# Expert tiles in groups of four, two and two rows, a new mix of step kinds, and two areas for tile outputs

## Time and profile before

| | us |
|---|---|
| median of 3 runs | 3298.54 (3296.21 to 3299.12) |
| profiled execution | 3306.1 |
| its span, first to last instruction | 3303.9 |
| mean granted TensorE clock | 0.959 |
| VectorE busy | 2989.0 (90%) |
| TensorE busy | 2864.8 (87%) |
| ScalarE busy | 2649.0 (80%) |
| GpSimd busy | 2656.7 (80%) |

### The profile page before, as it was taken

One profiled execution on the slowest core, in us unless ns is written; L12 is line 12 of the kernel. 1 busy time (PEld: TensorE's weight loads), 2 busy tenths in 40 slices (PEclk: granted clock), 3 DMA queues, 4 the chain that ended last, 5 costly groups with the idle time before them and its releaser, 6 DMA issues.

```text
span 3303.9 us, 58893 instructions
## 1 busy us (share of the span) xinstructions
PE 2864.8 (87%) x21429; PEld 2595.6 (79%) x21429; DVE 2989.0 (90%) x2141; ACT 2649.0 (80%) x6150; POOL 2656.7 (80%) x1289
## 2 busy tenths in 40 slices
PE   6889898988988799999868899989878879999676
PEld 5888888887877689888766788888767778899566
DVE  6999999999989999999999999999999999999610
ACT  6878888887978799898968689897977879988322
POOL 4889999888978898888988789797888878877501
PEclk8999999999999999999989899999989999999788
DMA  3342222222222335334221243524221143454176
GB/s 109 99 157 87 66 64 78 65 64 69 69 58 62 90 126 166 113 105 141 89 72 48 78 147 119 162 91 148 71 70 52 56 127 119 153 159 136 53 252 214
DMA packets 264660, 347.51 MB, mean 105 GB/s; under 512 B 88218, under 2 KB 157603, under 8 KB 263988
## 3 DMA queue, kind: packets, MB, share of 16 engines
q1 hardware_dynamic: 260418, 332.98, 32.5%
q0 software_dynamic: 3072, 8.39, 0.7%
q10 hardware_dynamic: 882, 2.38, 0.2%
HBM read 313.03 MB, written 30.62 MB: 104 GB/s over the span
## 4 chain that ended last, share of the span: by engine, by line
PE 33%; ACT 21%; DVE 17%; issue 14%; POOL 13%; DMA 2%; SPq 1%; DVEq 0%; POOLq 0%; ACTq 0%
POOL hC L1065 11%; ACT dA L1260 10%; DVE h L1292 9%; PE psY L1606 9%; PE psG L1545 8%; PE psX L1587 4%; DVE psX L1282 4%; PE psG L1632 4%; ACT xs L1231 3%; PE psX L1577 3%; PE psX L1545 2%; ACT gT L1114 1%; ACT hid L1215 1%; PE psX L1569 1%; DMA w_up<-in_w_exp 1%
## 5 line engine op out<-in xcount | busy, mean ns | idle before, releaser
L1065 POOL TENSOR_TENSOR hC<-h,cb 128x1024 f32<-128x1024 f32 x1024 | 2402.0, 2368 | 436.3 <-DVE h L1292 426.1
L1292 DVE TENSOR_TENSOR_SCAN h<-dA,psX 128x1024 f32<-128x1024 f32 (+1 forms) x1115 | 2303.7, 2101 | 83.4 <-ACT dA L1260 20.9
L1260 ACT ACTIVATE dA<-dt,negA 128x255 f32<-128x255 f32 x4096 | 1729.8, 510 | 180.1 <-DVE h L1292 178.4
L1606 PE MATMUL psY<-ident,hC 128*128 128x128 f32 x8192 | 1102.6, 279 | 47.9 <-DVE gT L1307 35.1
L1606 PEld LDWEIGHTS psY<-ident,hC 128*128 128x128 f32 x8192 | 956.3, 144 | 64.3 <-DVE gT L1307 38.2
L1282 DVE TENSOR_TENSOR psX<-dtu,psX 128x1024 f32<-128x1024 f32 x443 | 535.7, 1209 | 19.1 <-PE psX L1569 18.0
L1577 PE MATMUL psX<-ident,xs 128*128 128x128 f32 x2992 | 409.9, 282 | 115.2 <-ACT xs L1231 62.1
L1231 ACT ACTIVATE xs<-dtuT,bT 128x512 f32<-128x512 f32 x748 | 500.0, 723 | 1.3 <-PE psX L1577 1.2
L1577 PEld LDWEIGHTS psX<-ident,xs 128*128 128x128 f32 x2992 | 346.6, 145 | 169.4 <-ACT xs L1231 81.9
L1587 PE MATMUL psX<-diag_b,dtuT 128*128 128x128 f32 x3312 | 423.3, 282 | 39.2 <-DVE h L1292 37.4
L1587 PEld LDWEIGHTS psX<-diag_b,dtuT 128*128 128x128 f32 x3312 | 402.6, 197 | 68.5 <-issue 64.9
(11 more groups left out here) (213 smaller groups left out, 2056.7 us busy)
## 6 DMA issues: line engine op xcount, KB each, us to landing
cb<-c_dram SPq DMA_DIRECT2D x256, 512.0 KB
w_up<-in_w_exp SPq DMA_DIRECT2D x201, 256.0 KB, 3.1
w_down<-in_w_exp SPq DMA_DIRECT2D x201, 256.0 KB, 3.0
diag_b<-b_dram SPq DMA_DIRECT2D x207, 128.0 KB, 3.6
dA<-in_w_exp SPq DMA_DIRECT2D x39, 256.0 KB, 5.4
h<-in_w_exp SPq DMA_DIRECT2D x39, 256.0 KB, 5.2
x_slots<-got SPq DMA_DIRECT2D x16, 512.0 KB, 5.0
xg<-x_slots SPq DMA_DIRECT2D x60, 128.0 KB, 3.0
```

The costliest lines, as they stand in the source:

```text
L1065: eng.tensor_tensor(hC[i % NHC][:, :, :], h[i % NH][:, :, :], cw.to_broadcast([P, KI, L]), ALU.mult).then_inc(times_c, 1)
L1260: made = eng.activation(dA[j % NA][:, c, 1:L], dt[n % 2][:, c, 1:L], ACT.Exp, scale=negA[:, JOBS[n][0], c, s:s + 1])
L1292: made = eng.tensor_tensor_scan(h[i % NH][:, part, :].rearrange("p c t -> p (c t)"), dA[i % NA][:, part, :].rearrange("p c t -> p (c t)"), ...
L1606: made = eng.matmul(psY[:, tc, c * P:(c + 1) * P], hC[i % NHC][:, c, tc * P:(tc + 1) * P], ident[:, :], start=s == 0 and c == 0, stop=s == ...
```

## The change

The first ten jobs have the mix `EARLY`, the last six a new `LATE` with 26 P, 13 M and 25 T. Rows 0 to 3 are one group (23 tiles), rows 4 and 5 and rows 6 and 7 are two groups of 15. The slots of an area double (`SLOTS` = 8 * 1024), and `y_slots` becomes two areas by the group's parity, so that a group's first store waits only for the rows of the group before the last; 64 clearing DMAs of 512 KB replace 24. In the tail, the output tasks of rows 4 and 5 are taken from where they were put, and all set as one block behind the second product of the sixth tile of the last group.

```diff
-LATE = "PTPMPTPTPMTPTPT" * 4 + "PTPM"
+LATE = "PTMPT" * 12 + "PTMP"
-KINDS = FIRST_JOB + EARLY * 5 + LATE * (NJ - 6)
+KINDS = FIRST_JOB + EARLY * 9 + LATE * (NJ - 10)
...
-GROUPS = [[0, 1], [2, 3], [4, 5], [6, 7]]
+GROUPS = [[0, 1, 2, 3], [4, 5], [6, 7]]
...
+OUTPUTS = {"acc_load", "fetch", "fetched", "blend", "bn3", "norm3", "stored"}
...
                 task("tile_out", t, 0, "DMA", 2500, ("y_copy", t, 0),
-                     *((("fetched", GROUPS[g - 1][-1], 0),) if g and t == TILE0[g] else ()))]
+                     *((("fetched", GROUPS[g - 2][-1], 0),) if g > 1 and t == TILE0[g] else ()))]
...
         self.span = max(self.at.values())
+        late = [x for x in self.tail if x[1] in GROUPS[-2] and (x[0] in OUTPUTS or x[0] == "rstd" and x[2] == 2)]
+        rest = [x for x in self.tail if x not in late]
+        at = rest.index(("out", TILE0[-2] + 5, (1, 3))) + 1
+        self.tail = rest[:at] + late + rest[at:]
...
-        y_slots = nc.dram_tensor("y_slots", [SLOTS, D], F32, kind="Internal").ap()
+        y_slots = [nc.dram_tensor(f"y_slots{i}", [SLOTS, D], F32, kind="Internal").ap() for i in range(2)]
...
-        CLEARS = 3 * SLOTS * D // (P * KL * 2 * D)
+        CLEARS = 4 * SLOTS * D // (P * KL * 2 * D)
...
-                for b in GROUPS[g - 1] if g else ():
+                for b in GROUPS[g - 2] if g > 1 else ():
                     on.wait_ge(fetched[b], 16 * 4)
                 on.wait_ge(cleared, 16 * CLEARS)
-                eng.dma_start(y_slots[bass.DynSlice(tile_combo(t) * P, P), :], yg[:, :]).then_inc(y_tile_out, 16)
+                eng.dma_start(y_slots[g % 2][bass.DynSlice(tile_combo(t) * P, P), :], yg[:, :]).then_inc(y_tile_out, 16)
```

More of the change, by code:

```diff
@@ L751, in clear @@
             def clear(at):
-                tensor, part = (*x_slots, y_slots)[at // (CLEARS // 3)], at % (CLEARS // 3)
+                tensor, part = (*x_slots, *y_slots)[at // (CLEARS // 4)], at % (CLEARS // 4)
                 n = P * KL * 2
@@ L1026, in small_work @@
                             on.wait_ge(blended, KL * n)
-                        eng.indirect_dma_start(got_of[n][:, tc, k, :], None, y_slots, bass.IndirectOffsetOnAxis(slot_of[:, n, k, tc:tc + 1], 0),
+                        eng.indirect_dma_start(got_of[n][:, tc, k, :], None, y_slots[GROUP_OF[n] % 2], bass.IndirectOffsetOnAxis(slot_of[:, n, k, tc:tc + 1], 0),
                                                bounds_check=SLOTS - 1, oob_is_err=False).then_inc(fetched[n], 16)
```

## The result

The changed kernel takes **3343.9 us** (median of four runs, 3336.1 to 3345.4) against 3298.8 for the kernel before on the same chip (3296.2 to 3302.1): ratio 1.0132, 95% interval 1.0117 to 1.0147, slower by 45. I had forecast 3299 and a range of 3273 to 3324. All changed lines lie 6 further down (the scan L1292 is L1298, the gate L1307 is L1313, the transpose of a tile L1809 is L1815).

The account below looks back on a forecast made before the run. VectorE was taken to bound the steps, TensorE the work from job 10 to the last tile. Steps -61 and tail +61.8 (264.6 with the hold, against 202.8) gave +1, so 3299 against the median; range 3273 to 3324.

Parts of the forecast that it names:

- The steps, -61: Steps up to the last gate: 57 fewer plain steps save 69.0 on VectorE, less 8 for a stall; gate at 3040.
- the stall of 8: VectorE waiting for a late transposed fill in jobs 6 and 8, now early jobs: 8, bounds 0 and 16.
- TensorE becomes the bound: Rival, last six jobs: scans wait for fills, 30 of the gain is lost, 3329; chance 0.08.
- The tiles left, 11: Second group starts about step 26 of job 15, leaving 11 of its tiles in the tail beside 15 of the third.
- The tail, 246.6: Behind the steps: gate 1.3, row 7's work 20, mismatch 5, 26 tiles 188.5, start 6.9, end 24.9; hold extra.
- The eleven fill TensorE while row 7's chain waits: Tail: the second group's 11 tiles run beside row 7's attention, so TensorE bounds the tail from its start.
- My own sign of being wrong: End of the steps: a last gate later than 3060, where 3040, give or take 8, was forecast.
- My allowances behind the last scan: Tail terms beside tiles, row 7's work and the end: mismatched list times 5, start 6.9, SyncE hold 18, gate 1.3.
- The hold of SyncE, 18: Last group's sixth tile: loads and stores of rows 4 and 5 hold SyncE 22, costing 18, bounds 0 and 25.
- The clock: Tail: TensorE's granted clock near 1 from 3045 on, against 0.58 beside row 7's attention before.
- The window keeps the second group out: Rival, job 15: slow outputs leave 13 to 15 second-group tiles in the tail, +14 to +29, 3313 to 3328; chance 0.20.
- TensorE's total: Check on the sum: seven tiles fewer save 51, but 73 matrix steps for 57 plain and 16 scaled cost 108.

Follow-up runs that it names:

- the six other versions with the same order of work: Changed kernel plus tail edits: tiles held back 3334.5, outputs spread 3313.3, both 3312.2; then, cumulatively, single row loads 3304.1, no handicap 3291.5, rules from tile 30 3284.5.
- the version with the early half: Changed kernel's groups with ten jobs EARLY, old LATE, no tiles from step 1023 on, outputs of rows 4 and 5 in four pieces: 3279.3 (0.9933).
- the outputs spread: Changed kernel with the outputs of rows 4 and 5 in four pieces in place of one block: 3313.3 (1.0051).
- the last version of the tail: Changed kernel with tiles held back from step 1023, outputs in four pieces, single row loads, no handicap, last group's rules from tile 30: 3284.5 (0.9960).
- the late half of the mix: Kernel before with only the new LATE of 26 P in jobs 6 to 15: 3314.0 (1.0044).
- the seven versions with one order of work up to step 1022: The changed kernel (3343.9) and its six versions with only tail edits, 3334.5 down to 3284.5.

## Why the prediction was wrong

- **The steps, -61.** Up to job 14 the term held: jobs 6 to 9 took 49.5 less (738.5 against 788.0), more than the 38.7 of their 32 products; jobs 10 to 14 took 26.0 less (950.3 against 976.4), for 24.2 of 20 products; the stall of 8 didn't come (it was 8.1 once from 577 to 1143, as before). The last scan's end was forecast at 3035 and came at 3045.4. **This part failed in job 15**: 29 longer instead of 5 shorter (the six other versions with the same order of work took 212.2 to 215.7 there, the changed kernel 217.4). By the windows 8 of that is VectorE busy (192.7 against 184.6: three rows' outputs, which I had costed at none net in this sum, less the products), and 21 is idle: the waits for fills, 21.8 against about 1, of which I had priced none here, though the rival "TensorE becomes the bound" named them. TensorE waited 9.9 for weights in that job, and two of VectorE's waits, 8.3 in all, stand right behind such waits; the larger one (twice TensorE, then VectorE):

```profile
2947.81 2.08 PE L1638 MATMUL psG<-w_down,hid 128*128 128x256 f32 x4 [6.08 <-DMA w_down<-in_w_exp]
2950.11 1.91 PE L1583 MATMUL psX<-ident,xs 128*128 128x128 f32 x8
2952.06 2.29 DVE L1298 TENSOR_TENSOR_SCAN h<-dA,psX 128x1024 f32<-128x1024 f32 x1 [5.35 <-PE psX L1583]
```

SyncE was held 13.4 by the outputs' stores in the same stretch, and the version with the early half shows the same stretching in job 14, with the old late mix. So outputs among tiles can make fills late through SyncE; how far this holds for the changed kernel's 21.8, and what TensorE's matrix fills add, was not separated.
- **The tiles left, 11.** Right but for one: the second group started at step 30 of job 15 (I had 26), ten of its tiles were worked off behind the last scan. Of 26 transposes forecast behind the last gate 23 came there, since the gate itself was late. No tile ran before 1877, as forecast.
- **The tail, 246.6.** This is the step that failed: "The eleven fill TensorE while row 7's chain waits". Four ran ahead of the last sums and of row 7's first transposes at 12.8 each, and beside row 7's chain only two. I had counted how many tiles were left and taken for granted that the list sets them where TensorE is free. The list sets them by its own rules: no limit beside the last step, a handicap behind row 7's tasks beside the tail. Both stand in the code. Without the first 9.8 are gone, without the second 15.8 (table above). My own sign of being wrong, a last gate later than 3060, came: 3073.9. My allowances behind the last scan were 36.1 in all (5 mismatch, 6.9 start, 18 hold, 6.2 for the gate and its wait); the trace shows 70.7. With one tile fewer (-7.3) and the later scan (+10.3) that is the profile's 38 against my 1.
- **The hold of SyncE, 18.** Right: 22.3 on the queue and 17.6 on TensorE; with the outputs spread it is gone. The Trainium skill (DMA: Bandwidth & Descriptors, Anatomy of one DMA) says that a semaphore wait happens on the issuing sequencer before dispatch; the 22.3 agree with it. I had missed its twin, the pair load of tiles 38 and 39, 10.2 by the account and 9.1 by the run.
- **The clock.** I expected it near 1 from 3045 on; it was 0.93, 0.90 and 0.92 in the three stretches, and gaps remained in all of them. In the last version of the tail, from 3100.56 to 3240.6, it was 1.00, with TensorE busy 138.5 of 140.0.
- **The rivals.** "The window keeps the second group out" had the right sign and too low a price, and its mechanism didn't come: ten tiles, not 13 to 15. "TensorE becomes the bound" was true in part: the late half of the mix is slower by 16 by itself. I had weighed the mix as one edit; its halves have opposite signs. My range had no case in which the tail's tiles run at another rate than 7.25. TensorE's total, by which I had found the sum plausible, counts work and not waits: it could not show this.

## What to carry to other kernels

When work moves behind the last step of a pipeline, ask of each piece not only how long it takes but ahead of what it stands: a planner's rules that were harmless with little left over (no limit at the end, a handicap, the point from which the deep prefetch counts) decide where it lands. A trade between two engines (TensorE work for VectorE work) has to be priced stage by stage: here the same swap gains where TensorE has room and loses where it has not. And put no group of loads and stores that wait for one another into a queue that also feeds the bounding engine.

## What the runs showed of the hardware that was not expected

- The four tiles that waited for their weights took 12.8 each instead of 7.25, with three quarters held, at a DMA share of 0.59 and 190 GB/s. With nine held, undisturbed tiles drew 333 GB/s at a share of 0.97 in the kernel before (3163.3 to 3269.8) and 335 GB/s at 0.97 in the last version of the tail. The DMA engines could give more than they gave to the four, which points to the depth of the prefetch; no run changed that depth by itself. And at 7.25 a tile not only TensorE is full (102.9 busy of 106.5 in the kernel before): the DMA engines are too (0.97).
- Clears that took job 2's DMA share from 0.24 to 0.35 left its length at 174.0 to the tenth.
- The same instructions take times that lie in a band: 3290 to 3306 for 25 runs of the kernel before, 3276 to 3297 for ten of the last of the tail's versions, 3311 to 3331 for six of the one with spread outputs. In the traces of the seven versions with one order of work up to step 1022, a band of 17.4 is there already at the end of job 14, and 7.5 of it at the end of job 0, so a good part of it is there before the tail. The longer runs list a lower mean granted clock (spread outputs: 0.972 to 0.976 in the four up to 3313.9, 0.967 and 0.971 in the two of 3331). Which is cause and which effect was not found.
